# A transformer block on one core: routed rows carried as 16-bit halves, expert weights loaded in two pieces, one table value per routed tile

## The reference, cut to what matters

```python
# x: 2048 tokens x 256, float32
h = layernorm(x) * (1 + ca) + sa
x = x + ga * attention(h)      # 16 heads, latent keys (32) and rotated keys (64)
h = layernorm(x) * (1 + cb) + sb
# 32 experts, the 6 best of the 2 best of 4 groups of experts
scores = sigmoid(h @ gate_w)
weights, selected_experts = top 6, normalized
g, u = rows_of_expert @ w_gate, rows_of_expert @ w_up        # 256 -> 176
d = (silu(g) * u) @ w_down                                     # 176 -> 256
out = sum over the 6 experts of weights * d  +  shared expert
x = x + gb * out
```

## Time and profile before

| | |
|---|---|
| median of 3 runs | 1948.27 us (1947.77 to 1954.84) |
| profiled execution | 1951.45 us |
| its span, first to last instruction | 1949.6 us |
| busy share of the span | PE 95%, DVE 64%, ACT 71%, POOL 71% |
| mean granted clock of PE | 0.976 |
| start of attention | 115 us |
| start of routing | 1404 us |
| first and last routed tile on PE | 1565 and 1897 us |

### The profile page before, as it was taken

How to read it: one execution, slowest core, us unless ns; L and a number is a source line. 1 busy time by engine, 2 the same in 40 slices (tenths; PEclk the granted TensorE clock), 3 DMA queues, 4 the chain that set the end, 5 groups by cost and what they waited for, 6 DMA issues and landing times. The chain is left out here.

```text
span 1949.6 us, 43870 instructions
## 1 busy us (share of the span) xinstructions
PE 1851.4 (95%) x13730; PEld 981.7 (50%) x13730; DVE 1254.6 (64%) x2826; ACT 1384.7 (71%) x1908; POOL 1383.7 (71%) x837
## 2 busy tenths in 40 slices
PE   8979999999999999999999999999889689999986
PEld 6734444444444444444444444444376467777765
DVE  5777777767776777677767776776076345555553
ACT  5617888888888888888888888888752145555543
POOL 1526888988898889888988898889747723333330
PEclk9969999999999999999999999999999889999998
DMA  6100122112111211121112211000024379999979
GB/s 251 49 10 1 65 98 89 66 63 112 74 66 63 110 76 66 63 110 76 66 63 108 78 66 52 8 6 10 7 86 184 135 247 345 338 350 354 346 270 302
DMA packets 104645, 240.00 MB, mean 123 GB/s; under 512 B 24656, under 2 KB 57680, under 8 KB 104464
## 3 DMA queue, kind: packets, MB, share of 16 engines
q1 hardware_dynamic: 93840, 209.18, 30.2%
q0 software_dynamic: 10752, 30.16, 4.0%
HBM read 130.66 MB, written 104.37 MB: 121 GB/s over the span
## 5 line engine op out<-in xcount | busy, mean ns | idle before, releaser
L899 POOL TENSOR_TENSOR prob_lo<-prob,prob_hi 128x1024 f16<-128x1024 f32 x512 | 1080.8, 2129 | 166.4 <-ACT prob_hi L928 166.4
L974 DVE TENSOR_REDUCE maxes<-ring 128x1 f32<-128x512 f32 x1024 | 645.2, 684 | 232.4 <-PE ring L1065 229.9
L926 ACT ACTIVATE prob<-p_s,prob_scale 128x1024 f32<-128x1024 f32 x512 | 571.1, 1115 | 212.2 <-PE p_s L1084 190.7
L928 ACT ACTIVATE prob_hi<-p_s,prob_scale 128x1024 f16<-128x1024 f32 x512 | 570.3, 1114 | 0.0
L1065 PE MATMUL ring<-kr_hi,qr_hi 64*128 64x512 f16 x1024 | 374.8, 384 | 7.7 <-DVE qc_hi L961 4.2
L1065 PE MATMUL ring<-kc_pair,qc_hi 64*128 64x512 f16 x1024 | 371.3, 383 | 0.0
L1084 PE MATMUL p_s<-qr_lo,kr_hi 64*128 64x512 f16 x1024 | 287.0, 375 | 0.0
L1084 PE MATMUL p_s<-qr_hi,kr_lo 64*128 64x512 f16 x1024 | 286.5, 376 | 0.0
L1353 POOL DMA_INDIRECT ranked_out<-y,dest x128 | 123.1, 962 | 216.2 <-DVE y L1660 213.5
L1084 PE MATMUL p_s<-qr_hi,kr_hi 64*128 64x512 f16 x1024 | 244.2, 380 | 1.6 <-ACT prob_hi L928 1.6
L1084 PE MATMUL p_s<-qc_lo,kc_one 33*128 33x512 f16 x1024 | 242.4, 378 | 0.0
(11 more groups left out here) (248 smaller groups left out, 2447.4 us busy)
## 6 DMA issues: line engine op xcount, KB each, us to landing
w<-in_experts SPq DMA_DIRECT2D x128, 608.0 KB, 5.3
expert_rows<-zeros SPq DMA_DIRECT2D x129, 544.0 KB, 4.7
rows<-expert_rows SPq DMA_DIRECT2D x128, 136.0 KB, 4.7
got<-ranked_out SPq DMA_DIRECT2D x16, 768.0 KB, 10.4
wqb<-in_wqb SPq DMA_DIRECT2D x8, 768.0 KB, 4.9
recip_wide<-prob_recips SPq DMA_DIRECT2D x64, 64.0 KB
cbar<-att_t SPq DMA_DIRECT2D x64, 64.0 KB, 2.0
cbar<-in_woT SPq DMA_DIRECT2D x1, 2048.0 KB, 16.8
```

What stands on the lines that cost most here:

```text
L899: gp.tensor_tensor(prob_lo[s % NB][:, :], prob[s % 2][:, :], prob_hi[s % NB][:, :], ALU.subtract).then_inc(lo_ready, 1)
L926: act.activation(prob[s % 2][:, :], p_s[s % 2][:, :], ACT.Exp, bias=prob_scale[:, :], scale=SCALE / W_SCALE)
L928: act.activation(prob_hi[s % NB][:, :], p_s[s % 2][:, :], ACT.Exp, bias=prob_scale[:, :], scale=SCALE / W_SCALE).then_inc(p_ready, 1)
L974: best = v.tensor_reduce(maxes[:, at:at + 1], bank[:, :], AX.X, ALU.max)
```

## The change

It has six parts.

1. In setup, the last quarter's two high key parts are written by ACT rather than by POOL.
2. At the start of attention the copy of the first head's weights stands ahead of ACT's table load.
3. The table `tile_expert` is gone, with two DVE operations and half of a matmul. SP reads one value for each tile and takes the expert as that row number divided by 2048.
4. The experts' weights come as two transfers: 96 rows of 1216 values, and 32 rows of 704. The down weights use 88 rows, so the last 32 rows no longer carry padding. SP thus issues three transfers for each routed tile where it issued two.
5. Rows are scattered as two 16-bit halves in the same 1024 bytes. DVE normalizes into `normed` (which lies in the first four `w` buffers); ACT writes the high half of each tile ahead of its scaling, DVE the low half (`low_half`), for tiles 0 to 6 in the tile loop and for 7 to 15 in the shared expert's loop. Rows of a routed tile keep their size.
6. PE turns a routed tile's rows with four 16-bit matmuls against a 16-bit identity, two for each half of the columns, which sum the halves, in place of two 32-bit transposes.

```diff
+WROWS = 96
@@ setup, POOL
-                for part in (turned, slice(rest, rest + ROPE)):
-                    gp.tensor_copy(kr_hi[part, cols], kraw[turned, :]).then_inc(hi_ready, 1)
+                if q + 1 < QUARTERS:
+                    for part in (turned, slice(rest, rest + ROPE)):
+                        gp.tensor_copy(kr_hi[part, cols], kraw[turned, :]).then_inc(hi_ready, 1)
@@ setup, ACT, after the last quarter
+            act.wait_ge(kraw_ready, QUARTERS)
+            for base in (last_base, last_rest):
+                act.copy(kr_hi[base:base + ROPE, (QUARTERS - 1) * QC:QUARTERS * QC],
+                         kraw[last_base:last_base + ROPE, :]).then_inc(hi_ready, 1)
@@ attention, ACT
+            copy_wq(0)
             act.preload_act_table(ACT.Exp)
-            copy_wq(0)
@@ mixture, SP
             for n in range(2):
-                sp.dma_start(ws[n][:, :], a["experts"][E + n, :, :]).then_inc(ld_ws, 16)
+                sp.dma_start(ws[n][0:WROWS, :], a["experts_long"][E + n, :, :]).then_inc(ld_ws, 16)
+                sp.dma_start(ws[n][WROWS:P, 0:WIN], a["experts_short"][E + n, :, :]).then_inc(ld_ws, 16)
...
-            def load_weights(i, u):
-                e = sp.value_load(tile_expert[0:1, ds(i + u, 1)], min_val=0, max_val=E - 1)
+            def first_row(i, u):
+                return sp.value_load(tile_row[0:1, ds(i + u, 1)], min_val=0, max_val=E * S)
+
+            def load_weights(i, u, r):
+                e = ds(r // S, 1)
                 sp.wait_ge(y_mm, i + u + 1)
-                sp.dma_start(w[u][:, :], a["experts"][ds(e, 1), :, :].rearrange("a p n -> (a p) n")).then_inc(w_ld[u], 16)
+                sp.dma_start(w[u][0:WROWS, :], a["experts_long"][e, :, :].rearrange("a p n -> (a p) n")).then_inc(w_ld[u], 16)
+                sp.dma_start(w[u][WROWS:P, 0:WIN], a["experts_short"][e, :, :].rearrange("a p n -> (a p) n")).then_inc(w_ld[u], 16)
...
                 for u in range(U):
-                    load_weights(i, u)
-                    load_rows(i, u)
+                    r = first_row(i, u)
+                    load_weights(i, u, r)
+                    load_rows(i, u, r)
@@ mixture, ACT
                     act.wait_ge(t_mm, t - 1)
+                    act.copy(pairs[t - 2][:, 0:D], normed[t - 2])
                     modulate(h2T[:, (t - 2) * D:(t - 1) * D], p_t[t % 2], t_ready)
@@ mixture, DVE
-                v.tensor_scalar(hall[:, t * RW:t * RW + D], xt, mv[:, t * 2:t * 2 + 1], rstd[:, t:t + 1],
+                v.tensor_scalar(normed[t], xt, mv[:, t * 2:t * 2 + 1], rstd[:, t:t + 1],
                                 ALU.subtract, ALU.mult).then_inc(h_ready, 1)
+            def low_half(t):
+                v.wait_ge(t_ready, t + 1)
+                v.tensor_tensor(pairs[t][:, D:2 * D], normed[t], pairs[t][:, 0:D], ALU.subtract)
...
                 if t >= 1:
                     normalize(t - 1)
+                if 5 <= t < 5 + GROUP[END][0]:
+                    low_half(t - 5)
...
             for n in range(UNITS):
                 if n + 2 < UNITS:
                     shared_hid(n + 2)
+                for t in range(GROUP[END][0] + 2 * n, min(GROUP[END][0] + 2 * n + 2, T)):
+                    low_half(t)
@@ mixture, PE
+                pair = rows[u % U][:, 0:D].bitcast(F16)
                 for k in range(DK):
-                    last = pe.transpose(p_r[u % 2][:, k * P:(k + 1) * P], rows[u % U][:, k * P:(k + 1) * P], ident[:, :])
+                    for half in range(2):
+                        at = half * D + k * P
+                        last = pe.matmul(p_r[u % 2][:, k * P:(k + 1) * P], pair[:, at:at + P], ident16[:, :],
+                                         start=(half == 0), stop=(half == 1))
                 last.then_inc(r_mm, 1)
...
-                pe.wait_ge(w_ld[u % U], ring)
+                pe.wait_ge(w_ld[u % U], 2 * ring)
@@ host
+        "experts_long": np.concatenate([w_in[:, :WROWS], w_out], axis=2),
+        "experts_short": w_in[:, WROWS:],
```

More of the change, by code:

```diff
@@ L377, in _ @@
                     modulate(4 * q + 5)
+            last_base, last_rest = (QUARTERS - 1) % 2 * ROPE, QUARTERS % 2 * ROPE
+            act.wait_ge(kraw_ready, QUARTERS)
+            for base in (last_base, last_rest):
+                act.copy(kr_hi[base:base + ROPE, (QUARTERS - 1) * QC:QUARTERS * QC],
+                         kraw[last_base:last_base + ROPE, :]).then_inc(hi_ready, 1)
             for k in range(DK):
@@ L1203, in mixture @@
         tcol = sb("tcol", 4)
-        spread = sb("spread", 2 * P)
+        spread = sb("spread", P)
         own_slot = sb("own_slot", SLOT_TILES)
         tile_row = sb("tile_row", SLOT_TILES, I32, parts=1)
-        tile_expert = sb("tile_expert", SLOT_TILES, I32, parts=1)
         wsum = sb("wsum", T)
@@ L1273, in mixture @@
         ranked = [sem(f"ranked{n}") for n in range(U)]
+        ident16 = sb("ident16", P, F16)
+        normed = [w[t // 4][:, t % 4 * D:(t % 4 + 1) * D] for t in range(T)]
+        pairs = [hall[:, t * RW:t * RW + D].bitcast(F16) for t in range(T)]
         block = st.enter_context(nc.Block())
@@ L1292, in _, with load_rows @@
             for n in range(2):
-                sp.dma_start(ws[n][:, :], a["experts"][E + n, :, :]).then_inc(ld_ws, 16)
+                sp.dma_start(ws[n][0:WROWS, :], a["experts_long"][E + n, :, :]).then_inc(ld_ws, 16)
+                sp.dma_start(ws[n][WROWS:P, 0:WIN], a["experts_short"][E + n, :, :]).then_inc(ld_ws, 16)
             sp.wait_ge(answered, 2 * last + 2)
             store_heads(sp, last, scaling, cbar, stored)
-            def load_weights(i, u):
-                e = sp.value_load(tile_expert[0:1, ds(i + u, 1)], min_val=0, max_val=E - 1)
+            def first_row(i, u):
+                return sp.value_load(tile_row[0:1, ds(i + u, 1)], min_val=0, max_val=E * S)
+            def load_weights(i, u, r):
+                e = ds(r // S, 1)
                 sp.wait_ge(y_mm, i + u + 1)
-                sp.dma_start(w[u][:, :], a["experts"][ds(e, 1), :, :].rearrange("a p n -> (a p) n")).then_inc(w_ld[u], 16)
-            def load_rows(i, u, first=False):
-                r = sp.value_load(tile_row[0:1, ds(i + u, 1)], min_val=0, max_val=E * S)
+                sp.dma_start(w[u][0:WROWS, :], a["experts_long"][e, :, :].rearrange("a p n -> (a p) n")).then_inc(w_ld[u], 16)
+                sp.dma_start(w[u][WROWS:P, 0:WIN], a["experts_short"][e, :, :].rearrange("a p n -> (a p) n")).then_inc(w_ld[u], 16)
+            def load_rows(i, u, r, first=False):
                 if not first:
@@ L1306, in load_rows @@
                 sp.dma_start(rows[u][:, :], slots_dram[ds(r, P), :]).then_inc(row_ld[u], 16)
-            sp.wait_ge(tables, 2)
+            sp.wait_ge(tables, 1)
             for u in range(U):
-                load_weights(0, u)
+                load_weights(0, u, first_row(0, u))
             sp.wait_ge(scattered, 16 * TOPK * T)
             for u in range(U):
-                load_rows(0, u, first=True)
+                load_rows(0, u, first_row(0, u), first=True)
             with sp.Fori(1, SLOT_TILES // U) as trip_no:
@@ L1333, in _ @@
             gp.wait_ge(pads, 2)
-            gp.wait_ge(ld_ws, 32)
+            gp.wait_ge(ld_ws, 64)
             for n in range(2):
@@ L1564, in tile_table @@
                 step(v.tensor_scalar(tcol[:, 2:3], tcol[:, 2:3], float(E * S), None, ALU.min))
-                step(v.tensor_scalar(tcol[:, 3:4], tcol[:, 0:1], float(E - 1), None, ALU.min))
-                step(v.tensor_scalar(spread[:, 0:P], ident[:, :], tcol[:, 2:3], None, ALU.mult))
-                v.tensor_scalar(spread[:, P:2 * P], ident[:, :], tcol[:, 3:4], None, ALU.mult).then_inc(spread_ready, 1)
+                v.tensor_scalar(spread[:, :], ident[:, :], tcol[:, 2:3], None, ALU.mult).then_inc(spread_ready, 1)
             def keep_table():
@@ L1572, in keep_table @@
                 v.tensor_copy(tile_row[0:1, :], p_l[0:1, 0:P]).then_inc(tables, 1)
-                v.tensor_copy(tile_expert[0:1, :], p_l[0:1, P:2 * P]).then_inc(tables, 1)
             def weigh_tokens(j):
@@ L1586, in weigh_tokens @@
                 step(v.tensor_reduce(t3(weight, 8)[:, :, j], t3(pick), AX.X, ALU.add))
+            step(v.tensor_copy(ident16[:, :], ident[:, :]))
             v.wait_ge(col_mm, 1)
@@ L1698, in turn_h @@
                 for k in range(DK):
-                    last = pe.transpose(p_t[t % 2][:, k * P:(k + 1) * P], hall[:, t * RW + k * P:t * RW + (k + 1) * P],
-                                        ident[:, :])
+                    last = pe.transpose(p_t[t % 2][:, k * P:(k + 1) * P], normed[t][:, k * P:(k + 1) * P], ident[:, :])
                 last.then_inc(t_mm, 1)
@@ L1739, in spread_table @@
                 pe.wait_ge(spread_ready, 1)
-                pe.matmul(p_l[:, 0:2 * P], ones[:, :], spread[:, :], start=True, stop=True).then_inc(spread_mm, 1)
+                pe.matmul(p_l[:, 0:P], ones[:, :], spread[:, :], start=True, stop=True).then_inc(spread_mm, 1)
```

(9 more changed lines are left out.)

## The result

The changed kernel takes 2000.01 us (median of 4 runs, 1993.61 to 2002.76) against 1949.26 of the kernel before on the same chip: a ratio of 1.0243 as it stands on record, 95% interval 1.0222 to 1.0264 (the two medians alone give 1.026). It is slower by 2.4% where the prediction had 1942.1 and a range from 1938 to 1956. The profiled execution took 1993.61 us, its span is 1991.8 us.

What follows compares the result with a forecast made beforehand. SP's row issue, 2.580 us a tile against PE's 2.49, was taken to bound the routed tiles, with scatters and setup's end setting their start. Terms -3.4 + 1.7 - 7.4 + 2.9 = -6.2 gave 1942.1 us, range 1938 to 1956.

Steps and rivals of the forecast that it cites:

- Bytes: Routed tiles' transfers: 64 KB fewer read a tile, 2.5 us of transfer time to 2.3; needed, but given no sum.
- my rivals: Weight loads bound 16-bit turns (0.12), middle price (0.14), SP's third issue costs more (0.11), SP's pitch stays (0.13), low ends (0.10).
- the share: Sign in the routed tiles: the transfer engines' busy share falls from 0.98 to about 0.92.
- SP's pitch: Sign in the routed tiles: SP issues rows at or under 2.52 us a tile, where it took 2.580.
- A lead under the landing time: Sign: SP's lead at tile 127 stays over 5 us; falling under landing time would make SP the bound still.
- High key parts: Setup: two casts moved from POOL to ACT save 2.1 us; bounds -2.2 and -1.3 if POOL's copies slow.
- Table: Start of attention: weights copied ahead of ACT's table load save 1.3 us, at least 1.1.
- Making the halves: ACT copies and DVE subtractions for 16-bit rows delay the second group's slots: +1.7 us, bounds 1.2 and 3.15.
- SP's loop: Routed tiles: one reading fewer, one issue more, 2.58 to 2.51 us a tile; PE's lost 7.4 us come back.
- Turning: PE in routed tiles: four 16-bit matmuls at 0.060 us each for two transposes, +2.9 us; bounds -0.6 and +29.4.

Runs made afterwards that it cites:

- e10: e5 with 1088 of the 1216 weight columns loaded per routed tile, in one transfer of 128 rows; 2013.45 us, ratio 0.9934 against the kernel before.
- e2: The changed kernel with two weight transfers a tile, each of 128 rows (704 and 512 columns); 1953.99 us, ratio 1.0009.
- e13: e5 with the change's 96-row and 32-row weight transfers, so one table value a tile and no 16-bit halves; 1997.43 us, ratio 1.0216.
- e7: e1 with only the high half of the rows turned, two 16-bit matmuls a tile for four; 2015.57 us in one run.
- e1: The changed kernel with the weights again in one transfer of 128 rows; 1952.97 us, ratio 1.0003.
- e4: The changed kernel with two weight transfers of 64 rows each, whole width; 2047.56 us in one run.
- e5: The changed kernel without 16-bit halves and without the 96/32 split, rows turned in 32 bits; 2012.17 us, ratio 0.9929.
- e12: The kernel of e5 once more, on another chip; 2010.86 us, ratio 0.9930.
- e3: The kernel before with the weights in 96 and 32 rows and nothing else of the change; 2010.36 us, ratio 1.0293.

## Why the prediction was wrong

**The step that failed is *Bytes*.** It said that 64 KB fewer a tile bring the transfers from 2.5 to 2.3 us, that they "would then not bound a tile", and it gave them no sum. It priced a transfer by its bytes. The runs showed in its place: the same bytes in 128 rows do no harm (e10), all bytes in two transfers of 128 rows do none (e2), and 96 + 32 rows take 2.93 us a tile (e13) for what the full form does in 2.44 or less with more bytes (e7). In the changed kernel that is 2.886 - 2.533 = +0.35 us on e1's tile, 42 us. None of my rivals had it, though the change's fourth part names the 96 and 32 rows. The Trainium skill's section "Can I just issue two DMAs to hit both halves?" (SBUF — State Buffer) states that two transfers on the two halves gain next to nothing over one, and that only one transfer over all 128 partitions hits all 16 ports. The times agree with it: e4 is slow with two halves at 3.32 us a tile, e13 with 96 + 32 rows at 2.93, and e1 and e2 are not. None of these runs shows a port, so that part is the Trainium skill's word alone; what is shown is that the form of the transfer sets its cost.

The same step was wrong about before as well. It read 2.5 us of transfer time out of a share of 0.98. In e7 the engines bring the same 744 KB in 2.43 us, PE not waiting for them, at a share of 0.99 to 1.00, and in e10 fewer bytes leave it at 0.96 to 0.97:

```profile
1800.00:1850.00 50.00, 50.00 (x249) 37.46 (x248) 28.36 (x125) 28.58 (x83) 19.61 (x21) 1.00 0.99 365
```

Near 1 the share doesn't say how much is left. Two of the signs named ahead came out against the forecast, the share (1.05 for 0.92) and SP's pitch (2.89 us for 2.52); a third misleads. A lead under the landing time was to mean that SP is the bound, but here the lead is 9.7 us at tile 127, rows land in 10.4, and SP waits for PE.

**Point by point.** *High key parts*: -1.2 rather than -2.1; from `kraw` to its end POOL takes 8.28 us where it took 9.51. It came out near the lower bound, and by the way named there: POOL's first two copies took 1.12 and 1.07 us where two of 0.6 were counted, and they now lie beside DVE's work. *Table*: -1.1 rather than -1.3, from POOL's end to the projection 1.49 us where it was 2.60. *Making the halves*: 2.4 to 3.1 against 1.7, inside the bounds of 1.2 and 3.15 but at their upper end. *SP's loop*: 2.49 us of work against 2.51, right, and PE's waits did go in e1, which is the 7.4 us. *Turning*: each matmul 0.055 against 0.060, so this was nearer than asked; but 7.4 us against 2.9, as I priced the matmuls and not what stands behind them. In e1 it takes back all that the loop gives. The 81 ns a pair that the Trainium skill gives for a sustained stream (TensorE: Matmul & The Clock Gate, Back-to-back issue gap) do not show in these short runs of four: the pairs go at 55 ns.

With the sizes measured and the split taken out, the sum is -2.3 + 2.4 - 7.4 + 7.4 = +0.1 us, and e1 has 1.0003 +- 0.0014 times the kernel before. With the halves out as well it is -2.3 - 7.4 = -9.7, and e5 and e12 are 14 us faster on their chips. Of the whole kernels here it is the fastest against before: 0.993. On a chip of the first kind it wasn't run.

## What to carry to other kernels

Price a transfer by its form before its bytes: leave out padding only if each transfer still spans all 128 rows, and count what runs beside a bad one as slowed too. Cost an exchanged instruction together with the one behind it, which may have been hidden under the old one's length. A run that undoes one part must be costed on every engine as well, or, as in e3, it finds another bound and its time says nothing on the part.

## What the runs showed of the hardware

- The first tiles run at a clock that the change doesn't set. The first row turn comes at 1563.25 us in e1 and 1564.95 before, but the second tile's products take 2.72 us at e1's 1568.77 and 1.45 at 1570.55 before. PE had been idle for 17 and 23 us, and the granted clock in 1563 to 1575 us was 0.61 and 0.70, between the full 2.4 GHz and the level of 1.2 (e1 first, then before):

```profile
1563.00:1575.00 12.00, 9.79 (x35) 6.07 (x36) 1.03 (x4) 4.33 (x12) 0.00 (x0) 0.61 0.29 81
```

```profile
1563.00:1575.00 12.00, 7.79 (x25) 4.73 (x26) 0.72 (x3) 4.23 (x12) 0.00 (x0) 0.70 0.34 94
```

  The length of the idle time doesn't explain it. In e13 PE stands still for 23.1 us and starts at 1564.9, both as before, and the granted clock of the same 1563 to 1575 us is 0.51.

  From the first row turn to tile 8 it is 20.5 us before and 22.1 to 22.6 in the seven other kernels on these chips, with the change's parts and without. So the profiled execution of before was lucky by some 1.7 us, and that is why tile 8 comes 0.65 us later after the change.

- The chips of e5 to e12 lose their 70 us in one place, the shared expert's loop under POOL's scatters. PE's waits of 1450 to 1640 us in e12:

```profile
PE bank L1793 <- issue: 52.4, 4, 23.4
```

  Before has no such wait there on the first chip. The engines stand for up to 23 us without a releaser in the profile. Late instructions would fit; nothing here tests it.
